# Cross-attention of a decoder layer, pipelined over batches: the next batch is projected between the score steps, and its heads are stacked by transfers

## The reference, cut to what matters

```
q = layernorm(x1) @ Wq.T          # 4 batches x 512 rows x 512
k = context @ Wk.T ; v = context @ Wv.T   # k and v columns interleaved over the heads
q, k = rmsnorm per head (16 wide)
x2 = x1 + softmax(q k^T / 4) v    # per head, 512 x 512 scores
logits = layernorm(x2) @ router_weight    # for the experts' routing
```

## Time and profile before

| | |
|---|---|
| time, median of 3 | 1783.04 us (1779.92 to 1783.88) |
| time of the profiled execution | 1782.93 us |
| its span in the profile | 1781.1 us, so 1.8 us lie around it |
| cross-attention, from its first turned tile to its last logits | 530.25 to 1136.9 us |
| TensorE busy over the span | 83% |
| ScalarE busy | 59% |
| VectorE busy | 62% |
| GpSimd busy | 34%, in this stage next to nothing |

### The profile page before, as it was taken

The page is one execution under the profiler, slowest core; times in us unless marked ns, Lnnn a source line. Parts: engine busy times, 40 slices in busy tenths (PEclk is TensorE's granted clock), DMA queues, the critical chain, the costliest instruction groups (busy, mean ns, idle before and its releaser), DMA issues. The chain is left out here.

```text
span 1781.1 us, 30293 instructions
## 1 busy us (share of the span) xinstructions
PE 1478.7 (83%) x10066; PEld 1123.2 (63%) x10066; DVE 1109.2 (62%) x2035; ACT 1049.9 (59%) x2046; POOL 610.0 (34%) x436
## 2 busy tenths in 40 slices
PE   3988898988859798798887989435999999999990
PEld 2777676777747426525633842315899999999990
DVE  4667676667636426624813642577788888888880
ACT  3555455555534793694586479003677777777770
POOL 2444343444410000000000000021477777777772
PEclk9999999999979999999989989555899999999995
DMA  5000000000010002002002000421799999999986
GB/s 210 1 19 19 19 19 25 13 25 13 13 53 11 1 1 96 1 1 96 1 1 78 18 1 1 158 110 41 219 298 294 299 298 299 300 295 295 288 189 119
DMA packets 83620, 188.65 MB, mean 106 GB/s; under 512 B 13561, under 2 KB 13817, under 8 KB 83008
## 3 DMA queue, kind: packets, MB, share of 16 engines
q0 software_dynamic: 29248, 72.53, 18.3%
q1 hardware_dynamic: 53696, 113.74, 18.3%
q10 hardware_dynamic: 576, 0.98, 0.2%
HBM read 139.34 MB, written 55.05 MB: 109 GB/s over the span
## 5 line engine op out<-in xcount | busy, mean ns | idle before, releaser
L893 ACT ACTIVATE stage<-xa_ring 128x1024 f32<-128x1024 f32 x256 | 239.0, 1041 | 22.5 <-PE xa_ring L1115 22.5
L273 POOL TENSOR_TENSOR sa_prob<-sa_prob,sa_rinv 128x1024 f32<-128x1024 f32 x64 | 121.2, 1893 | 244.1 <-DVE sa_rinv L436 244.1
L793 POOL TENSOR_TENSOR xa_ve<-xa_mv,xa_eps 128x4 f32<-128x4 f32 x8 | 1.6, 200 | 581.0 <-DVE xa_mv L915 581.0
L1499 POOL DMA_INDIRECT ex_xg<-xn,token x128 | 172.1, 1345 | 82.9 <-issue 63.3
L331 ACT ACTIVATE sa_prob<-sa_sc_ps,sa_nmax 128x256 f32<-128x256 f32 x256 | 117.8, 473 | 110.9 <-DVE sa_nmax L423 110.9
L1127 PE MATMUL xa_out<-stage,xa_v 128*17 128x512 f32 x1024 | 139.7, 617 | 21.7 <-ACT stage L893 13.2
L72 PE MATMUL ex_ba<-ex_xh,ex_wh 128*128 128x256 f32 x512 | 150.6, 294 | 3.7 <-DVE ex_xl L1613 3.7
L74 PE MATMUL ex_ba<-ex_xh,ex_wl 128*128 128x256 f32 x512 | 145.8, 285 | 0.0
L73 PE MATMUL ex_ba<-ex_xl,ex_wh 128*128 128x256 f32 x512 | 145.7, 285 | 0.0
L1600 DVE TENSOR_TENSOR ex_wl<-ew_raw,ex_wh 128x1024 fp32r<-128x1024 f32 (+1 forms) x128 | 116.9, 955 | 35.9 <-ACT ex_wh L1543 35.9
L1031 DVE COPY xa_oT<-xa_out 128x512 f32<-128x512 f32 x32 | 22.1, 692 | 164.5 <-PE xa_out L1127 164.5
(11 more groups left out here) (222 smaller groups left out, 4295.1 us busy)
## 6 DMA issues: line engine op xcount, KB each, us to landing
ew_raw<-in_L_ffn_gate_proj_dram SPq DMA_DIRECT2D x64, 384.0 KB, 5.7
ew_raw<-in_L_ffn_up_proj_dram SPq DMA_DIRECT2D x64, 384.0 KB, 7.6
ew_rawd<-in_L_ffn_down_proj_dram SPq DMA_DIRECT2D x64, 256.0 KB, 5.1
ew_rawd<-in_L_ffn_down_proj_dram SPq DMA_DIRECT2D x64, 128.0 KB, 6.5
sa_x<-in_x_dram SPq DMA_DIRECT2D x16, 256.0 KB, 2.7
x<-sa_x SPq DMA_DIRECT2D x16, 256.0 KB, 2.0
stage<-in_ctx_dram SPq DMA_DIRECT2D x16, 256.0 KB, 3.4
stage<-x SPq DMA_DIRECT2D x16, 256.0 KB, 4.4
```

Source lines behind the costliest of these rows:

```text
L273: pool.tensor_tensor(prob[:, 4 * g:4 * g + 4, :], prob[:, 4 * g:4 * g + 4, :], rinv[:, 4 * g:4 * g + 4].unsqueeze(2).to_broadcast([P, 4, 2 ...
L893: act.activation(prob[:, u // 2 % 2, 2 * (u % 2):2 * (u % 2) + 2, :], ring[u % 3][:], ACT.Exp, scale=D2 ** -0.5).then_inc(s_ex[u % 3], 1)
L1499: pool.indirect_dma_start(out=xg[:, e % RING, j, :], out_offset=None, in_=xn3, in_offset=bass.IndirectOffsetOnAxis(token[:, at:at + 1], 0))\
```

## The change

`boundary` and `middle` are gone. One list of steps, `WALK`, is written out for every engine; 32 steps belong to the scores of each batch, and functions such as `begin`, `x_step` and `kn_step` give the step at which a piece of other work stands. TensorE's program for a step is: two pairs' scores, the values of the step before, all users of the one bank `b0` that fall on the step (turned sums, heads, tiles of x or context, router logits, routed tiles), and then a piece of a projection of the next batch (6 matmuls). Step w of batch b thus carries batch b + 1's projections; batch 0's are in the steps -36 to -9, and the last batch's scores have none.

The heads are no longer split before they are turned: `turn_heads` turns the four 128-wide blocks of the unsplit tile through `b0`, ScalarE and VectorE split the result into `hl`, SP stores both halves to a buffer in DRAM (`turned`), and when all eight tiles of a batch are there, 48 transfers in four groups of 12 (`load_turned(n, q)`) bring them into `kT` and `qT` in the stacked form, 16 partitions at a time. From batch 1 on, the head's factor is no longer rooted by ScalarE and multiplied by VectorE: VectorE copies the raw projection (`take_raw`), and GpSimd raises the mean square to the power -0.5 and multiplies (`heads`). `ring` has two slots rather than three, `xs` and `v` are doubled, context tiles have two slots rather than four, and `kT` and `qT` are zeroed beforehand by GpSimd.

```
@@ -621,45 +623,47 @@
-        v = m.sb("v", [P, T, H2, D2 + 1])
+        v = m.sb("v", [P, 2, T, H2, D2 + 1])
-        ring = [m.ps(f"ring{i}", [P, 2, D]) for i in range(3)]
+        ring = [m.ps(f"ring{i}", [P, 2, D]) for i in range(2)]
+        pr = m.ps("pr", [P, 2, D])
+        turned = nc.dram_tensor("turned", (2, 2, 2, D, S), F32).ap()
...
+            @block.gpsimd
+            def _(pool):
+                pool.memset(v[:, :, :, :, D2], 1.0).then_inc(w_z, 1)
+                pool.memset(kT[:].bitcast(F32), 0.0).then_inc(w_z, 1)
+                pool.memset(qT[:].bitcast(F32), 0.0).then_inc(w_z, 1)
+                pool.wait_ge(w_z, 3)
...
+        cx = stage[:, 8 * S:8 * S + 2 * D].rearrange("p (t d) -> p t d", t=2)
+        hl = stage[:, 8 * S + 2 * D:].bitcast(F32R).rearrange("p (i c q) -> p i c q", i=2, c=C)
+        xs = m.sb("xs", [P, 2, T, D])
...
+        def begin(n, j):
+            if j < T:
+                return STEPS * (n - 1) + 4 * j - 3
+            return STEPS * (n - 1) + (13 + 2 * (j - T) if n == 0 else (13, 16, 18, 21)[j - T])
+        def done(n, j):
+            return begin(n, j) + (3 if j < T else 1)
+        def kn_step(n, j):
+            return done(n, j) + (3 if n == 0 else 4)
+        def x_step(n, j):
+            return begin(n, j) - 1
+        def stats_step(n, t):
+            return begin(n, T) - 6 + t
+        def out_step(b, g):
+            return STEPS * b + T * g + 5
+        def rn_step(b, t):
+            return STEPS * (b + 1) + 3 + t
+        def rt_step(b, t):
+            return STEPS * (b + 1) + ((4, 8, 10, 14)[t] if b < B - 1 else 4 + t)
+        def rp_step(b, t):
+            return STEPS * (b + 1) + ((8, 10, 14, 15)[t] if b < B - 1 else 5 + t)
...
+        def uses_at(w):
+            return ([("out", b, g) for b, g in at(out_step, w, [(b, g) for b in range(B) for g in range(G)])]
+                    + [("kn", n, j) for n, j in at(kn_step, w, TILES)]
+                    + [("x", n, j) for n, j in at(x_step, w, TILES)]
+                    + [("logits", b, t) for b, t in at(rp_step, w, ROUTED)]
+                    + [("route", b, t) for b, t in at(rt_step, w, ROUTED)])
+
+        uses = [u for w in WALK for u in uses_at(w)]
...
+            def load_context(n, t):
+                before = (n, t - 2) if t >= 2 else (n - 1, t + 2)
+                if before[0] >= 0:
+                    sp.wait_ge(s_b0, USE["x", *before] + 1)
+                sp.dma_start(cx[:, t % 2], context[n * T + t]).then_inc(ld_c[t], 16)
+            def store_turned(n, j):
+                sp.wait_ge(s_free, USE["kn", n, j] + 1)
+                for part in range(2):
+                    sp.dma_start(turned[n % 2, j // T, part, :, j % T * P:(j % T + 1) * P].rearrange("(c p) t -> p c t", p=P),
+                                 hl[:, part].bitcast(F32)).then_inc(st_h, 16)
+            def load_turned(n, q):
+                sp.wait_ge(st_h, 32 * (n + 1) * KQ)
+                if n > 0:
+                    for i in range(2):
+                        sp.wait_ge(s_sc[i], STEPS * (n - 1) + 2 * T * (q + 1))
+                for side, where in enumerate((kT, qT)):
+                    rows = turned[n % 2, side].rearrange("a (pair i d) t -> a i d pair t", i=2, d=D2)
+                    for i in range(2):
+                        for r, part in enumerate((0, 1, 0) if side == 0 else (0, 0, 1)):
+                            at_row = i * W2 + r * D2
+                            sp.dma_start(where[at_row:at_row + D2, 4 * q:4 * q + 4, :].bitcast(F32),
+                                         rows[part, i, :, 4 * q:4 * q + 4, :]).then_inc(ld_h[q], 16)
...
+            for w in WALK:
+                for n, t in at(lambda n, t: x_step(n, t) - 4, w, [(n, t) for n in range(1, B) for t in range(2)]):
+                    load_context(n, t)
+                for n, t in at(lambda n, t: x_step(n, t - 2), w, [(n, t) for n in range(B) for t in range(2, T)]):
+                    load_context(n, t)
+                for n, j in at(kn_step, w, TILES):
+                    store_turned(n, j)
+                for n in range(B):
+                    if w == kn_step(n, KQ - 1):
+                        for q in range(3):
+                            load_turned(n, q)
+                    if w == STEPS * n:
+                        load_turned(n, 3)
...
+            def heads(n, j):
+                k = number(n, j) - KQ
+                i = k % 2
+                pool.wait_ge(s_ms, KQ + k + 1)
+                pool.tensor_tensor(power[:, i], ms[:, i], half[:], ALU.pow).then_inc(s_pw, 1)
+                pool.wait_ge(s_pw, k + 1)
+                pool.wait_ge(s_raw, k + 1)
+                pool.tensor_tensor(kn[:, i], kn[:, i], power[:, i].unsqueeze(2).to_broadcast([P, H2, D2]),
+                                   ALU.mult).then_inc(s_kp, 1)
...
+            def exponentials(w):
+                for i in range(2):
+                    act.wait_ge(s_sc[i], w + 1)
+                    at_least(act, s_pv, w - 1)
+                    act.activation(prob[:, w % 2, 2 * i:2 * i + 2, :], ring[i][:], ACT.Exp, scale=D2 ** -0.5).then_inc(s_ex[i], 1)
...
+                elif kind == "kn":
+                    k = number(b, j)
+                    at_least(act, st_h, 32 * k)
+                    act.activation(hl[:, 0], b0[:], ACT.Copy).then_inc(s_high, 1)
...
+            def take_raw(n, j):
+                k = number(n, j) - KQ
+                dve.wait_ge(s_b0, USE["kn", *divmod(k - 2 + KQ, KQ)] + 1)
+                if j < T:
+                    dve.wait_ge(s_vv, 2 * (n * T + j) + 2)
+                for src, hs in sources(n, j):
+                    last = dve.tensor_copy(kn[:, k % 2, hs], src)
+                last.then_inc(s_raw, 1)
...
+            def bank_free(kind, b, j):
+                if not own_bank(kind, b):
+                    at_least(pe, s_free, USE[kind, b, j])
...
+            def turn_heads(n, j):
+                k = number(n, j)
+                pe.wait_ge(*((s_kd, j + 1) if n == 0 else (s_kp, k - KQ + 1)))
+                bank_free("kn", n, j)
                 i = j % 2
+                for c in range(C):
+                    last = pe.transpose(b0[:, c, :], kn[:, i, 8 * c:8 * c + 8, :].rearrange("p h d -> p (h d)"), ident[:])
+                last.then_inc(s_b0, 1)
...
+                    before = last_on_banks(n, j)
+                    if before is not None:
+                        if before < KQ:
+                            pe.wait_ge(s_kd, before + 1)
+                        else:
+                            pe.wait_ge(s_raw, before - KQ + 1)
+                            pe.wait_ge(s_vv, before // KQ * 2 * T + 2 * min(before % KQ + 1, T))
...
+            for w in WALK:
+                if 0 <= w < STEPS * B:
+                    scores(w)
+                if 0 <= w - 1 < STEPS * B:
+                    values(w - 1)
+                for kind, b, j in uses_at(w):
+                    if kind == "out":
+                        turn_out(b, j)
+                    elif kind == "kn":
+                        turn_heads(b, j)
+                    elif kind == "x":
+                        turn_x(b, j)
+                    elif kind == "logits":
+                        project_route(b, j)
+                    else:
+                        turn_route(b, j)
+                for n, j in TILES:
+                    step = w - begin(n, j)
+                    if 0 <= step < (C if j < T else 2):
+                        project(n, j, step)
```

More of the change, by code:

```diff
@@ L740, in product_bank @@
[L740 to L750 removed]
+        scaled = m.sb("scaled", [P, T, 4, D2])
+        route_h = m.sb("route_h", [P, C, P], F32R)
+        route_l = m.sb("route_l", [P, C, P], F32R)
@@ new lines, in uses_at @@
+        def uses_at(w):
[5 more added lines that the diff above has]
+        uses = [u for w in WALK for u in uses_at(w)]
+        USE = {u: i for i, u in enumerate(uses)}
```

701 lines of the change are left out of this document (302 added, 399 removed).

## The result

The changed kernel takes 1855.05 us (median of 4, 1844.58 to 1865.47) against 1783.46 for the kernel before: 4.1% slower, ratio 1.0406, 95% interval [1.0345, 1.0467]. Predicted were 1824 us and a range of 1745 to 1890.

A forecast was written before the change was run, and what follows sets the result against it. TensorE was to become the bound, but transfers decide: 50.9 lost at the start + 354.5 for steps + 79.1 of stalls - 445.6 + 2 = +40.9 on 1782.93, so 1824 us; range 1745 to 1890.

The forecast's parts named there:

- steps of three batches: Score steps of batches 0 to 2: 106.9 + 2 x 120.3, plus 7 for TensorE's lower clock, 354.5 us.
- stalls at the changes of batch: TensorE waiting for loads and context tiles at later changes of batch: 2 x 35.7 + 7.7 = 79.1 us.
- L: Queue time of one 128 KB load of heads to 16 partitions, taken as 1.2 us; forecast span 0.9 to 1.5.
- 120L - 103: Whole kernel's change in us as a function of one load's cost; no change at 0.86 us a load.
- 36L + 2.7: Before batch 0's scores: 36 loads plus 2.7 us for the context tile behind them, at 1.2 us a load.
- 36L - 7.5: Step 0 of batches 1 and 2: TensorE's wait for the context tile behind 36 loads, 35.7 us each.
- 12L - 6.7: Later changes of batch: wait of the first scores for the first 12 loads, 7.7 us.
- Term (a): One bank `b0`: a second turn in a step waits 2.1 us in steps 4, 8, 12; 3.5 together in 17 and 21.
- (d): Batches 1 and 2: the previous batch's routing also uses `b0`, 13.4 us instead of the bare 7.0, 120.3 us a batch.
- the last batch's steps are as before ..., 2 us more: Last batch's scores: two slots make both scores of a step wait for the exponentials just ahead, 2 us more.
- GpSimd as the bound: Rival: GpSimd's power at twice its price, 11.8 us a tile, costs 13 us a batch, 1863 us; chance 0.06.
- Loads that are nearly hidden: Rival: loads move at SP's pace of 0.43 us each, 1733 us; chance 0.28.

The follow-up runs named there:

- experiments 1 and 2: Changed kernel with the next batch's context tiles 0 and 1 issued ahead of the loads: 1797.97 us; then with the loads also spread nearer their use: 1775.19 us.
- experiment 8: Kernel with context tiles first and loads spread, the first three heads of batches 1 to 3 turned one step earlier: 1760.68 us, ratio 0.9858.
- experiment 10: Kernel before the change, with the changed kernel's 8 MB DRAM buffer added and 128 KB stored to it once: 1788.45 us, ratio 1.0009.
- experiment 3: Changed kernel without the 192 loads of the stacked heads and the waits for them: 1755.58 us, ratio 0.9837.
- experiment 7: Kernel with context tiles first and loads spread, GpSimd's power replaced by a product: 1778.56 us, ratio 0.9946.
- experiment 4: Changed kernel with each 128 KB load going to 64 partitions instead of 16: 1824.14 us, ratio 1.0228.

## Why the prediction was right, and where its terms were off

The terms of the sum against the trace, in us:

| term | predicted | measured |
|---|---|---|
| first exponential of batch 0 later than 602.2 | 50.9 | 649.8 - 602.2 = 47.6 |
| steps of three batches | 354.5 | 429.7 - 53.7 = 376.0 |
| stalls at the changes of batch | 79.1 | 2.65 + 19.87 + 3.16 + 19.73 + 8.29 = 53.7 |
| three batches of before | -445.6 | -445.6 |
| last batch and what follows, to the routing stage | 2 | 112.7 - 94.3 = 18.4 |
| experts | 0 | 654.1 - 639.1 = 15.0 |
| sum | 40.9 | 65.2 (the rows, rounded, give 65.1) |

**L, the cost of a load.** Predicted 1.2 us, measured 0.82: from the first load's issue at 608.8 to the turn of the context tile at 640.9, less a landing of 2.7, over 36. It was the term on which the chances stood, and it lay below the break-even of 0.86 that the sum gave, while the kernel was 4.1% slower. With 0.82 the prediction's own 120L - 103 gives 4.6 us faster. So the mechanism that it named is the one the trace shows, but that the sign and the size came out is in part luck: L was 46 us too dear (120 x 0.38), and the other terms were together 70 us too low. Those are the steps (21.5), the last batch (16.4), the experts (15), the start beyond its 36L (10.4) and the changes of batch beyond their loads (6.5), each taken up below. The nearest row was a load that shared the queue, and taking 45% of 2.1 us gave 0.95; I then raised it to 1.2 for the narrowness, and that step failed. The page "SBUF — State Buffer" of the Trainium skill (section "Door 1: The DMA port swizzle") gave 104 GB/s for partitions 0 to 15, and nearly the same rate for 32 partitions as for 64. The second the trace bears out (226 and 232 GB/s). For 16 partitions 142 to 161 were measured; these loads stand one behind the other in the queue and go in turn to six ranges of 16, so it is not the page's single transfer. A range of 48 partitions, which by its table reaches as many ports as 64, moved 163, so in these runs the width alone doesn't give the rate.

**Before batch 0.** The form 36L + 2.7 was right, with 32.1 us of it where 45.9 were predicted. But the first load could be issued, behind the last store's landing, only at 608.8 and not at 600.4: each of the four queries' tiles was waited for by 1.7 to 3.0 us, since `normalise_query` comes one step before its turn, a wait the prediction did not have (9.3 us in all, where the first load came 8.4 late). The 6.8 us behind the context tile were 8.9, as TensorE stood at the clock of 0.50 (1.2 GHz) after 38.7 us of idling: its turn took 1.11 us instead of 0.66, and the first six projection matmuls 2.73 us instead of 1.38.

**At a change of batch.** With L = 0.82 the prediction's 36L - 7.5 is 22.0 us; the trace has 22.5 and 22.9. Its 12L - 6.7 is 3.1; the first wait in batches 1 and 2 is 2.65 and 3.16. Batch 3 waited 8.29, because the last steps of batch 2 carry no further batch's projection, so its first step comes sooner; so the program says, no run tried it. The place, the tile and the order of the waits were as said, and experiments 1 and 2 show that they are the queue's order.

**The steps.** 112.5, 133.5 and 130.0 us for batches 0 to 2, where 106.9, 120.3 and 120.3 were predicted, plus 7 for the clock. The sum, 376, is 6% above the 354.5. Term (a) is confirmed by experiment 8, as an average over nine places. A step with a projection only was taken as 2.8 us and is 3.1 to 3.6. The surplus over batch 0, the routing, was put at 13.4 us and is 20.9 and 17.5; step 4 of batch 1, with three users of the bank, takes 9.1 us where 8 were predicted. The trace shows no one place for the rest; it wasn't tried apart.

**The last batch.** The failed step is "the last batch's steps are as before ..., 2 us more". Batch 3's scores also carry batch 2's routing, as (d) says of batches 1 and 2. From its first exponential to the last one's end it is 77.2 us against 65.0 before, and from there to the routing stage 35.5 against 29.2. Of the 12.2 us some 4 are the two slots: where nothing but scores is left, four steps take 8.47 us instead of 7.98 before, so 0.12 us a step where 2 us in all were predicted. The other 8 stand in the first half of the batch, with the routing. Behind the last exponential, batch 3's own four routed tiles stand 5.1 us apart at a clock of 0.56.

**The experts.** Not foreseen at all, and not explained. Twelve profiles of kernels with the change have 645.8 to 655.5 us behind the routing stage's start; the kernel before and the one of experiment 10 have 639.1 and 639.2. The time is lost in the experts' loop, TensorE being idle before the first product of some experts (19 times, 0.7 us, in the changed kernel's trace between 1370 and 1800) for nothing that the profile shows. It isn't chance: before, all experts are 7.57 us apart; in each of the twelve profiles the distance grows at the same four places, from the 8th, the 24th, the 40th and the 56th one on, mostly to between 7.8 and 9.2 us, and falls back after one to ten experts (four of the profiles have one more such place). Neither the loads (experiment 3 has 648.2) nor the buffer's place causes it; what is left is the longer, written-out program or the way in which the loop is entered, and that wasn't tried.

**The rivals.** GpSimd as the bound is out (experiment 7; its power took 5.43 us, 5.2 was predicted). Loads that are nearly hidden gave 1733 us in the prediction, yet with none at all the kernel took 1755.6. So no cheaper load could have given 1733: the start, the steps, the last batch and the experts cost what the sum did not have.

## What to carry to other kernels

When work is moved onto a shared queue, ask of every small transfer that an in-order engine will wait for which large ones stand ahead of it: 256 KB behind 4.7 MB cost three stalls of 20 to 39 us, and issuing two tiles of each batch earlier made the kernel 57 to 60 us faster. When a resource with one slot (here one bank) is used by two chains of steps, offset the chains: a change of one in a step number gave 15 to 18 us. And when a table of steps puts one batch's work into the next, price the last batch too, for it still carries what its predecessor left.

## What the runs showed of the hardware

Loads of 128 KB in 2 KB pieces, many in the queue, kept the transfer engines full at 142 to 161 GB/s to 16 partitions with four pieces each, and at 226 to 232 GB/s to 32 with two or 64 with one. One of 384 KB to 48 partitions, four pieces to each, moved only 163. SP's issue of a load took 0.46 to 0.48 us to 16 partitions and 0.63 to 64; in experiment 4 it held the transfer engines to 0.70 of their time. ScalarE loaded its table anew (1.28 us) right before the first exponential of batch 0 in the changed kernel, at 648.49, in line with the first scores.
